# A Mamba-2 mixer on one core: one convolution tap of B and C moved to GpSimd, and eight smaller edits

## The chip, the cores and the metric

The kernel runs on one core of a Trainium2 chip. The core has five engines that each work through their own instruction list and wait for one another by semaphores: PE (TensorE, the matrix engine; PEld is its weight load), DVE (VectorE), ACT (ScalarE), POOL (GpSimd) and SP, which here only issues DMA transfers. Work that several engines share goes through SBUF (the 128-partition memory) and PSUM (8 banks of 128 x 512 float32, written by PE, not readable by POOL). The metric is the device time of one execution in microseconds (us).

## What is computed

```python
x  = hidden_states                                 # 2 x 512 tokens x 512
xn = layernorm(x)
out = x + mamba2(xn) + ffn(xn)
# mamba2: 128 heads of 64, state 128, 8 groups of B and C, causal conv of 4 taps, chunks of 128 tokens
gate, hBC, dt = split(xn @ in_proj_w.T)            # 8192, 8192 + 2*1024, 128
hs, B, C = split(silu(conv4(hBC) + conv_b))        # each channel: 4 taps along the tokens
dt = softplus(dt + dt_bias); A = -exp(A_log)
y = chunked state-space scan(hs*dt, A*dt, B, C) + D*hs
y = y * silu(gate); y = rmsnorm over each eighth of the 8192 channels (8 groups) * norm_weight
mamba2 = y @ out_proj_w.T
# ffn: xn @ W.T + b, plus one of 4 low-rank updates per token (ranks 8..64), chosen by a softmax gate
```

All matrix products of the projections are done in three passes over split operands: `xTh`, `wh` hold rounded values (fp32r), `xTl`, `wl` what the rounding left.

## The kernel before

The kernel is a hand-written program with one instruction list per engine, in which every order is the order of the code. For each of the two batches `b` (512 tokens, held as 4 chunks of 128, index `j`) it goes through these stages.

- **First tokens.** DVE computes mean and variance (`stats`, `mv`, `ve`), POOL the inverse deviation (`rstd`), DVE the normalized tokens `xn` (their memory is that of `gt`, so the trace calls them gt). PE turns them into PSUM (`turn_tokens`), ACT and DVE split them into `xTh` and `xTl` (`token_hi`, `token_lo`). For the second batch this is done inside the last steps of the first.
- **dt, gate of the feed-forward part, feed-forward part.** PE projects `dt` (`project_dt`) and the low-rank part (`project_ag`); DVE computes the softplus by a series with one multiply-add per coefficient (`soft_log`, constant `SERIES`) and the choice of rank (`route`), whose result `um` PE turns for ACT to copy (`uT`). `project_ffn` is 48 matmuls into the four output banks `bo`.
- **The B/C stage.** A loop over the 8 groups `g`. PE projects B of the group (unit u = 0, bank `bh` or `bt`) and C (u = 1, bank `bg` or `by`). The convolution of a unit is: ACT writes the newest tap with the bias from PSUM to `cv[:, u]` (`last_tap`), DVE adds the three older taps to it (`tap`, L820), ACT writes the tanh half of the silu to the PSUM bank (`tanh_conv`, L307), DVE multiplies (`silu_conv`, L826) into `h2` (B) or `ct` (C). Then PE multiplies B and C (`scores`, L640, one bank, `bo[2]`) and turns B (L644), and DVE masks the scores (`mask_scores`, L960) into `gt`. Two things order this loop: `cv` has two halves, one for B and one for C, so `last_tap` waits until the silu of the same half of the group before has read it; and `scores` waits for the mask of the scores before, since both use `bo[2]`:

```python
def last_tap(un, u, src):
    act.wait_ge(v_h2, did(un - 2))
...
def scores(b, g):
    pe.wait_ge(v_h2, did(b * UNITS + 2 * g + 1))
    pe.wait_ge(v_g, did(n - 1))
```

- **The 64 steps.** A loop over `m`, software-pipelined over three values of m: PE projects two heads and their gate (24 matmuls, L583), forms the output of step m-2 (12 matmuls, L726), the states, the scan and the turned channels of step m-1 (L770, L778, L786, L798). After each 8 steps (a norm group, `PER_GROUP`) the four banks `bo` hold the group's part of the output: DVE scales and adds two of them to `acc` (`add_group`, L846), ACT scales the other two into `part` (`drain`, L339) and POOL adds those (`add_drained`, L505).

SP issues loads in the order of the code too; weights of the B/C stage and of the steps pass through a two-deep buffer `raw`, from which ACT makes `wh` (`split_hi`) and POOL `wl` (`split_lo`).

Of the kernel before, what the change touches and what calls it, by code (L numbers as in the profile page):

```python
# [13 lines left out]
P = 128  # L14
# [17 lines left out]
SERIES = [1.0 / (2 * k + 1) for k in range(8)]  # L32
# [12 lines left out]
PRO_DVE_LOG = PRO_DVE_XT + 12  # L45
PRO_DVE_SC = PRO_DVE_LOG + 4
PRO_DVE_UM = PRO_DVE_SC + 16
PRO_DVE_CS = PRO_DVE_UM + 3
PRO_DVE_DTT = PRO_DVE_CS + 1
PRO_DVE_DTD = PRO_DVE_DTT + 1  # L50
PRO_DVE = PRO_DVE_DTD + NJ
CONST, SCALED = 6, 3
# [3 lines left out]
def mixer_kernel(nc, x, w_step, w_bc, w_dtag, w_out, par, headpar, w_ffn, w_b, b_ffn, b_gate, out):  # L56
    with ExitStack() as ctx:
# [57 lines left out]
        part = sb("part", [P, 2, HID])  # L115
# [28 lines left out]
        csT, dtT, ecT = xg[:, 0], xg[:, 1], tg[:, :]  # L144
        dec, dtd = yo[:, :], S[:, :, :].rearrange("p c k -> p (c k)")
# [8 lines left out]
        ld_const, const_ok, scaled = sem("ld_const"), sem("const_ok"), sem("scaled")  # L154
# [42 lines left out]

        def dtag(b):

            return b * LOADS  # L200
# [12 lines left out]

        block = ctx.enter_context(nc.Block())

        @block.sync
        def _(sp):
# [5 lines left out]
            load_x(0)  # L223
            sp.dma_start(par_sb[:, :, :], par).then_inc(ld_const, 16)
            sp.dma_start(hp[:, :], headpar).then_inc(ld_const, 16)
            for h in range(2):
                sp.dma_start(w_b_sb[MAXR * h:MAXR * (h + 1), :], w_b).then_inc(ld_const, 16)
            sp.dma_start(b_row[:, :], b_ffn.unsqueeze(0).broadcast_to([P, HID])).then_inc(ld_const, 16)
            sp.dma_start(bg_row[:, :], b_gate.unsqueeze(0).broadcast_to([P, NR])).then_inc(ld_const, 16)
# [7 lines left out]
            def store(b):  # L237
                last = b * GROUPS + (GROUPS - 1)
                blocks = out[b].rearrange("(j p) d -> p j d", p=P)
                if b + 1 < NB:  # L240
                    sp.wait_ge(v_acc, did(last, 2))
                    sp.wait_ge(p_acc, did(last, 2))
                    sp.dma_start(blocks, acc[:, b, :, :]).then_inc(st_out, 16)
                else:
                    for j in range(NJ):
                        sp.wait_ge(v_acc, did(last, 2, j + 1))
                        sp.dma_start(blocks[:, j, :], acc[:, b, j, :]).then_inc(st_out, 16)

            load(dtag(0))
            for b in range(NB):  # L250
                sp.wait_ge(a_ex, did(b * STEPS - 1))
                sp.dma_start(raw_f, w_ffn).then_inc(ld_ffn, 16)
                if b == 0:
                    load(bc(0, 0))
                load(bc(b, 1))
                if b == 0:
                    load_x(1)
# [33 lines left out]
        def _(act):  # L291
            start(act, (a_dr, a_tap, a_th, a_tg, a_rl, a_ex, a_s1, a_xh, a_sq, a_wh, a_wn, a_woh, a_bt))
            act.wait_ge(ld_const, 96)
# [11 lines left out]
            def tanh_conv(un, u, dst):  # L305
                act.wait_ge(v_tap, did(un, 3))
# [39 lines left out]
            for b in range(NB):  # L346
# [8 lines left out]
                if b == 0:  # L355
                    split_ffn(0)
# [769 lines left out]
```

## Time and profile before

| | |
|---|---|
| median of 3 runs | 1664.31 us (1662.31 to 1664.91) |
| the profiled execution | 1666.25 us, its span from first to last instruction 1664.5 us |
| mean granted TensorE clock | 0.994 of full speed |
| busy share of the span | PE 98%, PEld 82%, DVE 84%, ACT 75%, POOL 68% |
| HBM traffic | 207 MB read, 126 GB/s over the span |

In the profile's rows a timeline line gives the start, the busy time of one or several instructions in a row, the engine, the line of the kernel, the operation, the tiles it writes and reads, the count, and in brackets how long the engine had been idle and who released it. Times are us from the start of the span.

### The profile page before, as it was taken

The numbers are of one execution on the slowest core, as the hardware profiler recorded it, in microseconds if no ns is written. First come the engines' busy times: TensorE is split into PE (matmuls) and PEld (weight loads), VectorE is DVE, ScalarE is ACT, GpSimd is POOL, SyncE is SP. The second block draws the span as 40 slices with busy tenths as digits, with TensorE's granted clock in tenths as the row PEclk, the third lists the DMA queues.
The fourth block names the chain that finished last, engine by engine and source line by source line (L and its number), as shares of the span: only waits on it lengthen the run. The fifth ranks groups of instructions, "written<-read, shape, count | busy, mean of one in ns | idle before, by whom it ended". The sixth has DMA issues, their size and how long they took to land.

```text
span 1664.5 us, 28889 instructions
## 1 busy us (share of the span) xinstructions
PE 1625.2 (98%) x9638; PEld 1357.8 (82%) x9638; DVE 1394.8 (84%) x2361; ACT 1253.7 (75%) x2474; POOL 1130.0 (68%) x1442
## 2 busy tenths in 40 slices
PE   6999999999999999999899999999999999999998
PEld 4778888888888888888777788888888888888886
DVE  6888888888888888888879888888888888888887
ACT  3478788787888787887735787878887887878784
POOL 5237776767776777767653487777677777677674
PEclk9999999999999999999999999999999999999999
DMA  4244444344444344444313444444444444434431
GB/s 156 76 135 130 127 145 133 123 146 126 130 146 129 129 144 132 124 146 125 117 39 114 145 125 132 145 127 129 146 123 133 143 128 130 146 123 134 146 112 59
DMA packets 82307, 212.17 MB, mean 127 GB/s; under 512 B 11120, under 2 KB 27504, under 8 KB 81904
## 3 DMA queue, kind: packets, MB, share of 16 engines
q1 hardware_dynamic: 82160, 210.33, 40.0%
q8 instruction: 78, 1.28, 0.3%
q14 instruction: 69, 0.57, 0.1%
HBM read 207.14 MB, written 3.15 MB: 126 GB/s over the span
## 4 chain that ended last, share of the span: by engine, by line
PE 91%; DVE 4%; POOL 2%; ACT 1%; issue 1%; DMA 0%; SPq 0%; ACTq 0%; DVEq 0%; POOLq 0%
PE bg L583 21%; PE bo L726 21%; PE bt L583 11%; PE bh L583 11%; PE by L778 7%; PE bg L798 6%; PE bh L770 3%; PE bt L770 2%; PE bh L786 2%; PE bt L786 2%; DVE cv L820 1%; PE by L583 1%; PE bo L583 1%; PE bo L640 1%; PE bg L705 1%
## 5 line engine op out<-in xcount | busy, mean ns | idle before, releaser
L549 POOL TENSOR_TENSOR xl<-xg,xh 128x256 fp32r<-128x256 f32 x254 | 291.5, 1169 | 351.5 <-ACT xh L407 350.3
L483 POOL TENSOR_TENSOR wl<-raw,wh 128x256 fp32r<-128x256 f32 x584 | 424.3, 757 | 112.7 <-ACT wh L298 112.7
L311 ACT ACTIVATE mt<-cs_row,cs_tok 128x128 f32<-128x128 f32 x1024 | 324.6, 391 | 0.0
L563 POOL TENSOR_TENSOR wol<-raw_o,woh 128x256 fp32r<-128x256 f32 x256 | 181.4, 730 | 40.9 <-ACT woh L441 40.9
L726 PE MATMUL bo<-woh,xh 128*128 128x512 f32 x512 | 201.8, 394 | 2.1 <-POOL xl L549 2.1
L1034 DVE TENSOR_TENSOR mt<-mt,gt 128x1024 f32<-128x1024 f32 x128 | 202.8, 1584 | 0.4 <-ACT mt L450 0.4
L726 PE MATMUL bo<-woh,xl 128*128 128x512 f32 x512 | 200.9, 392 | 0.0
L726 PE MATMUL bo<-wol,xh 128*128 128x512 f32 x512 | 200.8, 392 | 0.0
L820 DVE SCALAR_TENSOR_TENSOR cv<-bt,par_sb,cv 128x511 f32<-128x511 f32 (+2 forms) x216 | 160.9, 745 | 12.4 <-ACT cv L302 7.3
L820 DVE SCALAR_TENSOR_TENSOR cv<-bh,par_sb,cv 128x511 f32<-128x511 f32 (+2 forms) x216 | 160.9, 745 | 6.7 <-ACT cv L302 1.6
L556 POOL TENSOR_TENSOR sqa<-sqa,sq 128x256 f32<-128x256 f32 x222 | 159.0, 736 | 1.2 <-ACT sq L424 1.2
L298 ACT ACTIVATE wh<-raw 128x1024 fp32r<-128x1024 f32 (+1 forms) x146 | 152.1, 1042 | 0.7 <-DMA raw<-in_w_dtag 0.7
L407 ACT ACTIVATE xh<-xg 128x512 fp32r<-128x512 f32 x128 | 81.0, 633 | 94.6 <-DVE xg L1011 94.6
L583 PE MATMUL bg<-xTh,wh 128*128 128x512 f32 (+1 forms) x552 | 148.2, 390 | 1.6 <-DVE yo L1003 1.6
L583 PE MATMUL bg<-xTh,wl 128*128 128x512 f32 (+1 forms) x552 | 147.9, 390 | 0.0
L583 PE MATMUL bg<-xTl,wh 128*128 128x512 f32 (+1 forms) x552 | 147.6, 389 | 0.0
L778 PE MATMUL by<-mt,xt 128*64 128x128 f32 x2032 | 139.0, 279 | 0.0
L450 ACT ACTIVATE mt<-mt 128x1024 f32<-128x1024 f32 x128 | 135.5, 1058 | 4.1
L583 PEld LDWEIGHTS bg<-xTh,wh 128*128 128x128 f32 (+1 forms) x552 | 102.8, 187 | 23.5 <-issue 1.3
L583 PEld LDWEIGHTS bg<-xTl,wh 128*128 128x128 f32 (+1 forms) x552 | 103.2, 187 | 22.0
L583 PEld LDWEIGHTS bg<-xTh,wl 128*128 128x128 f32 (+1 forms) x552 | 103.2, 187 | 22.0
L726 PEld LDWEIGHTS bo<-woh,xh 128*128 128x128 f32 x512 | 96.4, 188 | 30.0 <-POOL xl L549 3.8
(179 smaller groups left out, 3549.1 us busy)
## 6 DMA issues: line engine op xcount, KB each, us to landing
raw<-in_w_step SPq DMA_DIRECT2D x128, 512.0 KB, 3.5
cs_row<-cs_rows SPq DMA_DIRECT2D x128, 512.0 KB, 5.4
raw_o<-in_w_out SPq DMA_DIRECT2D x128, 256.0 KB, 4.0
ec_row<-ec_rows SPq DMA_DIRECT2D x256, 96.0 KB, 4.7
raw<-in_w_bc SPq DMA_DIRECT2D x16, 512.0 KB, 3.5
acc<-in_x SPq DMA_DIRECT2D x4, 512.0 KB, 4.7
cs_row<-in_w_ffn SPq DMA_DIRECT2D x2, 1024.0 KB, 5.9
out_dram<-acc SPq DMA_DIRECT2D x1, 1024.0 KB, 6.2
```

Of the source, the lines that this page charges most:

```text
L298: act.activation(wh[:, n % 2, 0:width(n)], raw[:, n % 2, 0:width(n)], ACT.Copy).then_inc(a_wh, 1)
L311: e = act.activation(mt[:, m % 2, h, chunk(j)], cs_row[:, m % 2, h, chunk(j)], ACT.Relu, bias=cs_tok[:, j, 2 * m + h:2 * m + h + 1], scale ...
L450: act.activation(mt[:, u], mt[:, u], ACT.Exp, scale=-1.0).then_inc(a_ex, 1)
L483: e = pool.tensor_tensor(wl[:, n % 2, cols], raw[:, n % 2, cols], wh[:, n % 2, cols].bitcast(F32), ALU.subtract)
L549: e = pool.tensor_tensor(xl[:, u, cols], xg[:, u, cols], xh[:, u, cols].bitcast(F32), ALU.subtract)
L556: e = pool.tensor_tensor(sqa[:, cols], sqa[:, cols], sq[:, cols], ALU.add)
L563: e = pool.tensor_tensor(wol[:, 1 - u, cols], raw_o[:, 1 - u, cols], woh[:, 1 - u, cols].bitcast(F32), ALU.subtract)
L583: mm = pe.matmul(dst, a(k), c(k), start=(n == 0 and k == 0), stop=(stop and n == 2 and k == KT - 1))
L726: mm = pe.matmul(bo[j][:, :], a[:, u, chunk(j)], c[:, u, :], start=(first and k == 0), stop=False, skip_group_check=True)
L778: mm = pe.matmul(yb[HD * h:HD * (h + 1), chunk(j)], xt[:, j, HD * h:HD * (h + 1)], mt[:, 1 - u, h, chunk(j)], start=True, stop=True)
L820: dve.scalar_tensor_tensor(out=cv[:, u, k:], in0=src[:, 0:L - k], scalar=par_sb[:, un % UNITS, TAPS - 1 - k:TAPS - k], in1=cv[:, u, k:], o ...
L1034: dve.tensor_tensor(mt[:, 1 - u], mt[:, 1 - u], gt[:, (m - 1) % GROUPS, :].unsqueeze(1).broadcast_to([P, 2, L]), ALU.mult).then_inc(v_m, 1)
```

## The change

It has nine parts.

1. **B/C taps.** In the B/C stage, ACT writes two taps instead of one: the newest into `cv[:, u]`, the second newest into a buffer of its own (`tap2`, the memory of `sq` and `sqa`). POOL adds the second to the first (`add_tap`), and DVE adds only the two oldest (`far_taps`), behind POOL. The steps keep the old way.
2. **Order in the B/C loop.** On DVE the silu of C of group g-1 now stands behind the far taps of B of group g, and the mask of group g-3 behind that; on ACT the tanh of C of group g-1 stands behind the two taps of B of group g. `decays` moves from g = 0 to g = 1 and `decays_to_end` from g = 1 to g = 3.
3. **Series.** `SERIES` has 6 coefficients instead of 8: two DVE operations on 512 columns fewer per batch.
4. **First loads.** SP loads the first weights before the parameters; the parameters have three semaphores of their own instead of one. `scale_consts` moves on POOL from the start to behind `split_ffn_lo`.
5. **Four banks.** The first batch's turned tokens go to `bo[0..3]`, so PE does not wait for the split of the first two; ACT splits the feed-forward weights earlier.
6. **Pre-multiplied identity.** PE does 12 matmuls of the identity with itself before its first wait.
7. **Norm of the second batch.** Its statistics were one block of DVE work at m = 61 and its `norm` two pairs at m = 62 and 63; now they are single instructions, in the steps m = 52 to 57 and m = 60 to 63, ahead of the state update.
8. **Three output blocks by ACT.** `DVE_BLOCKS = 1`: DVE adds one of the four blocks, ACT scales three, POOL adds three (two in one step and the third in the next).
9. **Last step.** In the last batch DVE takes the tokens and masks the decays of the last step ahead of the y chain.

The core of the diff:

```diff
-SERIES = [1.0 / (2 * k + 1) for k in range(8)]
+SERIES = (1.0, 0.33333333660263703, 0.1999985316596525, 0.14296178997116357, 0.10853287901120869, 0.11612164608329507)
+TOP = len(SERIES) - 1
+DVE_BLOCKS = 1
+ACT_BLOCKS = NJ - DVE_BLOCKS
+        tap2 = sq, sqa
...
# scalar
+            def two_taps(b, g, u, src):
+                un = b * UNITS + 2 * g + u
+                last_tap(un, u, src)
+                if g == 0 and u == 0:
+                    act.wait_ge(p_sqa, squares(b - 1, STEPS - 1))
+                elif g == 0:
+                    act.wait_ge(t_ss, did(b * GROUPS - 1))
+                else:
+                    act.wait_ge(p_cv, did(bc_unit(b, g - 1, u)))
+                act.activation(tap2[u][:, :], src[:, :], ACT.Identity,
+                               scale=par_sb[:, un % UNITS, TAPS - 2:TAPS - 1]).then_inc(a_t2, 1)
...
-                act.wait_ge(p_acc, did(g - 1, 2))
-                for j in (2, 3):
-                    act.activation(part[:, j - 2, :], bo[j][:, :], ACT.Identity, scale=rr[:, j:j + 1]).then_inc(a_dr, 1)
+                act.wait_ge(p_acc, did(g - 1, ACT_BLOCKS))
+                for j in range(DVE_BLOCKS, NJ):
+                    act.activation(part[:, j - DVE_BLOCKS, :], bo[j][:, :], ACT.Identity, scale=rr[:, j:j + 1]) \
+                        .then_inc(a_dr, 1)
...
                 for g in range(GROUPS):
                     act.wait_ge(t_b, did(b * GROUPS + g))
-                    last_tap(b * UNITS + 2 * g, 0, bank_b[g % 2])
+                    two_taps(b, g, 0, bank_b[g % 2])
+                    if g >= 1:
+                        tanh_bc(b, g - 1, 1, bank_c[(g - 1) % 2])
+                    if g >= 3:
+                        take_b(b, g - 3)
                     act.wait_ge(t_c, did(b * GROUPS + g))
-                    last_tap(b * UNITS + 2 * g + 1, 1, bank_c[g % 2])
+                    two_taps(b, g, 1, bank_c[g % 2])
                     split_hi(bc(b, g + 2))
...
-                    tanh_conv(b * UNITS + 2 * g, 0, bank_b[g % 2])
-                    tanh_conv(b * UNITS + 2 * g + 1, 1, bank_c[g % 2])
+                    tanh_bc(b, g, 0, bank_b[g % 2])
# gpsimd
             def scale_consts():
                 pool.wait_ge(scaled, 1)
+                pool.wait_ge(ld_par, 32)
...
+            def add_tap(b, g, u):
+                pool.wait_ge(a_t2, did(bc_unit(b, g, u)))
+                for cols in (slice(1, 257), slice(257, L)):
+                    e = pool.tensor_tensor(cv[:, u, cols], cv[:, u, cols],
+                                           tap2[u][:, cols.start - 1:cols.stop - 1], ALU.add)
+                e.then_inc(p_cv, 1)
...
                     inverse_dev(0)
-                    pool.wait_ge(ld_const, 96)
-                    scale_consts()
                     split_lo(dtag(0))
-                if b == 0:
                     split_lo(bc(0, 0))
                     split_ffn_lo(0, 0)
                 split_ffn_lo(b, 1)
+                if b == 0:
+                    scale_consts()
...
-                for g in range(2, GROUPS):
-                    split_lo(bc(b, g))
+                for g in range(GROUPS):
+                    for u in range(2):
+                        add_tap(b, g, u)
+                    if g + 2 < GROUPS:
+                        split_lo(bc(b, g + 2))
# tensor
+            for i in range(WARM):
+                pe.matmul(by[:, chunk(i % NJ)], ident[:, :], ident[:, :], start=True, stop=True)
...
-                    mm = pe.transpose(bank_t[j % 2][:, chunk(k)], xn[:, j, chunk(k)], ident[:, :])
+                    mm = pe.transpose(bank_x(b, j)[:, chunk(k)], xn[:, j, chunk(k)], ident[:, :])
# vector
+            def far_taps(b, g, u, src):
+                q, un = bc_unit(b, g, u), b * UNITS + 2 * g + u
+                for k in (2, 3):
+                    if k == 2:
+                        dve.wait_ge(p_cv, did(q))
+                    else:
+                        dve.wait_ge(v_bc, did(q, 2, 1))
+                    dve.scalar_tensor_tensor(out=cv[:, u, k:], in0=src[:, 0:L - k],
+                                             scalar=par_sb[:, un % UNITS, TAPS - 1 - k:TAPS - k], in1=cv[:, u, k:],
+                                             op0=ALU.mult, op1=ALU.add).then_inc(v_bc, 1)
...
-                    for k in range(1, TAPS):
-                        tap(un, 0, bank_b[g % 2], k)
-                    for k in range(1, TAPS):
-                        tap(un + 1, 1, bank_c[g % 2], k)
+                    far_taps(b, g, 0, bank_b[g % 2])
+                    if g >= 1:
+                        silu_conv(un - 1, 1, bank_c[(g - 1) % 2], ct[:, g - 1, :])
+                    if g >= 3:
+                        mask_scores(b, g - 3)
+                    far_taps(b, g, 1, bank_c[g % 2])
...
                     silu_conv(un, 0, bank_b[g % 2], h2[:, g % 2, :])
-                    silu_conv(un + 1, 1, bank_c[g % 2], ct[:, g, :])
-                    if g == 0:
+                    if g == 1:
+                        add_lora(b)
                         decays(b)
-                    if g >= 2:
-                        mask_scores(b, g - 2)
...
+                    ahead = m == STEPS and b + 1 == NB
+                    if ahead:
+                        take_tokens()
+                        mask_decays()
...
+                    if b + 1 < NB and STEPS - 12 <= m < STEPS - 6:
+                        h, part_of = divmod(m - (STEPS - 12), 3)
+                        if part_of < 2:
+                            stats_of(b + 1, 2 * h + part_of)
+                        else:
+                            variance(b + 1, h)
+                    if b + 1 < NB and STEPS - NJ <= m < STEPS:
+                        norm(b + 1, m - (STEPS - NJ))
```

How DVE's list stands at group g = 2 of the first batch before the change (cv is the convolution buffer, h2 and ct are B and C after the silu, gt the masked scores; the wait names are semaphores, a_ of ACT, v_ of DVE, p_ of POOL, t_ of PE):

```order
L820 SCALAR_TENSOR_TENSOR cv<-bh,par_sb,cv 128x511 [waits a_tap]
L820 SCALAR_TENSOR_TENSOR cv<-bh,par_sb,cv 128x510 [waits v_tap]
L820 SCALAR_TENSOR_TENSOR cv<-bh,par_sb,cv 128x509 [waits v_tap]
L820 SCALAR_TENSOR_TENSOR cv<-bg,par_sb,cv 128x511 [waits a_tap]
L820 SCALAR_TENSOR_TENSOR cv<-bg,par_sb,cv 128x510 [waits v_tap]
L820 SCALAR_TENSOR_TENSOR cv<-bg,par_sb,cv 128x509 [waits v_tap]
L826 SCALAR_TENSOR_TENSOR h2<-bh,cv 128x512 [waits a_th,t_bt]
L826 SCALAR_TENSOR_TENSOR ct<-bg,cv 128x512 [waits a_th]
L960 TENSOR_TENSOR gt<-bo2,causal 128x512 [waits t_gm]
```

The same place on DVE with the change (groups 2 and, from bt on, 3):

```order
L880 SCALAR_TENSOR_TENSOR cv<-bh,par_sb,cv 128x510 [waits p_cv,pro_dve]
L880 SCALAR_TENSOR_TENSOR cv<-bh,par_sb,cv 128x509 [waits v_bc]
L896 SCALAR_TENSOR_TENSOR ct<-by,cv 128x512 [waits a_th]
L880 SCALAR_TENSOR_TENSOR cv<-bg,par_sb,cv 128x510 [waits p_cv]
L880 SCALAR_TENSOR_TENSOR cv<-bg,par_sb,cv 128x509 [waits v_bc]
L896 SCALAR_TENSOR_TENSOR h2<-bh,cv 128x512 [waits a_th,t_bt]
L880 SCALAR_TENSOR_TENSOR cv<-bt,par_sb,cv 128x510 [waits p_cv]
L880 SCALAR_TENSOR_TENSOR cv<-bt,par_sb,cv 128x509 [waits v_bc]
L896 SCALAR_TENSOR_TENSOR ct<-bg,cv 128x512 [waits a_th]
L1037 TENSOR_TENSOR gt<-bo2,causal 128x512 [waits t_gm]
```

Each unit has lost its first tap, the first of the two left waits for POOL (p_cv), the two silus are no longer neighbours, and the mask stands in the group after.

ACT's list at group g = 2 of the first batch, before:

```order
L302 ACTIVATE cv<-bh,par_sb 128x512 [waits v_h2,t_b]
L302 ACTIVATE cv<-bg,par_sb 128x512 [waits v_h2,t_c]
L298 ACTIVATE wh<-raw 128x1024 [waits ld_raw1]
L307 ACTIVATE bh<-cv 128x512 [waits v_tap]
L307 ACTIVATE bg<-cv 128x512 [waits v_tap]
```

and with the change (sq and sqa are the memory of the second tap):

```order
L320 ACTIVATE cv<-bh,par_sb 128x512 [waits v_h2,t_b]
L337 ACTIVATE sq<-bh,par_sb 128x512 [waits p_cv]
L342 ACTIVATE by<-cv 128x512 [waits v_bc]
L320 ACTIVATE cv<-bg,par_sb 128x512 [waits v_h2,t_c]
L337 ACTIVATE sqa<-bg,par_sb 128x512 [waits p_cv]
L316 ACTIVATE wh<-raw 128x1024 [waits ld_raw1]
L342 ACTIVATE bh<-cv 128x512 [waits v_bc]
```

The second tap has come in behind the first, and the tanh of C of group 1 (by) has moved behind the taps of B of group 2.

POOL's list at the same place had only the four pieces of `wl` per group (L483); with the change two units of two additions stand between them:

```order
L522 TENSOR_TENSOR wl<-raw,wh 128x256 [waits a_wh]
L522 TENSOR_TENSOR wl<-raw,wh 128x256 x3
L529 TENSOR_TENSOR cv<-cv,sq 128x256 [waits a_t2]
L529 TENSOR_TENSOR cv<-cv,sq 128x255
L529 TENSOR_TENSOR cv<-cv,sqa 128x256 [waits a_t2]
L529 TENSOR_TENSOR cv<-cv,sqa 128x255
```

So POOL now stands between ACT's taps and DVE's for every unit.

## Rows read from the trace of the kernel before

**Rows 1.** Windows: PE, PEld, DVE, ACT, POOL busy (count), PEclk, DMA share, GB/s.
```profile
110.00:800.00 690.00, 689.46 (x4192) 579.13 (x4191) 583.55 (x995) 555.46 (x1111) 503.51 (x633) 1.00 0.43 134
```

**Rows 2.** Timeline of PE, the step after a norm group's end.
```profile
209.11 1.17 PE L583 MATMUL bh<-xTh,wh 128*128 128x512 f32 x4
...
219.72 1.41 PE L798 MATMUL bg<-ct,S 128*128 128x128 f32 x6
220.89 1.17 PE L583 MATMUL bt<-xTh,wh 128*128 128x512 f32 x4
...
232.06 1.17 PE L583 MATMUL bh<-xTh,wh 128*128 128x512 f32 x4
```

**Rows 3.** Timeline of DVE, then of ACT, in that step.
```profile
212.26 1.40 DVE L846 SCALAR_TENSOR_TENSOR acc<-bo,rr,acc 128x512 f32<-128x512 f32 x2
...
219.61 0.98 DVE L853 SCALAR_TENSOR_TENSOR S<-S,cd_bc,bt 128x64 f32<-128x64 f32 x4 [0.70 <-ACT S L444]
...
211.85 1.24 ACT L339 ACTIVATE part<-bo,rr 128x512 f32<-128x512 f32 x2
```

**Rows 4.** Timeline of ACT, then of DVE, B/C stage, group 2.
```profile
61.13 0.78 ACT L302 ACTIVATE cv<-bh,par_sb 128x512 f32<-128x512 f32 x1 [3.04 <-DVE h L826]
...
64.17 2.31 DVE L820 SCALAR_TENSOR_TENSOR cv<-bg,par_sb,cv 128x511 f32<-128x511 f32 x3
...
67.75 0.68 DVE L960 TENSOR_TENSOR gt<-bo,causal 128x512 f32<-128x512 f32 x1
```

**Rows 5.** The page, part 5: a two-input addition on POOL.
```profile
L556 POOL TENSOR_TENSOR sqa<-sqa,sq 128x256 f32<-128x256 f32 x222 | 159.0, 736 | 1.2 <-ACT sq L424 1.2
```

**Rows 6.** Timeline of PE, B/C stage: first batch, then second.
```profile
60.49 1.16 PE L640 MATMUL bo<-ct,h 128*128 128x128 f32 x8 [1.66 <-DVE acc L985]
...
64.58 1.07 PE L583 MATMUL by<-xTh,wh 128*128 128x512 f32 x4
...
881.25 2.08 PE L640 MATMUL bo<-ct,h 128*128 128x128 f32 x8 [3.19 <-DVE acc L985]
...
888.08 1.07 PE L583 MATMUL by<-xTh,wh 128*128 128x512 f32 x4
```

**Rows 7.** Windows behind two idle stretches of PE.
```profile
33.60:37.00 3.40, 3.40 (x10) 2.68 (x9) 2.72 (x11) 1.48 (x4) 1.64 (x3) 0.53 0.19 36
...
881.20:887.20 6.00, 5.96 (x20) 5.20 (x21) 5.55 (x9) 2.99 (x4) 2.80 (x4) 0.51 0.00 0
```

**Rows 8.** Timeline of DVE, then of PE, first batch before the steps.
```profile
22.77 0.43 DVE L895 TENSOR_SCALAR mt<-mt 128x512 f32<-128x512 f32 x1 [7.38 <-ACT mt L331]
...
29.23 4.37 DVE L904 SCALAR_TENSOR_TENSOR bt<-bt,sg 128x512 f32<-128x512 f32 x6
...
38.27 2.98 DVE L935 TENSOR_TENSOR gt<-ag,msk 128x64 f32<-128x64 f32 x4
...
48.12 0.68 DVE L942 SCALAR_TENSOR_TENSOR sg<-tg,mt 128x512 f32<-128x512 f32 x1
...
50.62 0.43 DVE L948 TENSOR_SCALAR xg<-sg 128x512 f32<-128x512 f32 x1
...
57.95 2.48 DVE L985 TENSOR_TENSOR acc<-bo,acc 128x512 f32<-128x512 f32 x4
...
60.95 0.68 DVE L826 SCALAR_TENSOR_TENSOR ct<-by,cv 128x512 f32<-128x512 f32 x1
...
32.52 1.20 PE L583 MATMUL bo<-xTh 128*128 128x512 f32 x4 [3.29 <-POOL xTl L494]
...
109.23 1.18 PE L583 MATMUL bt<-xTh,wh 128*128 128x512 f32 x4
```

**Rows 9.** Timeline of PE, steps 62 and 63 of the first batch.
```profile
799.62 1.17 PE L583 MATMUL bh<-xTh,wh 128*128 128x512 f32 x4
...
813.68 1.17 PE L583 MATMUL bt<-xTh,wh 128*128 128x512 f32 x4
```

**Rows 10.** Timeline of PE, last step.
```profile
1647.30 0.91 PE L770 MATMUL bt<-xd,btok 128*128 128x128 f32 x6 [3.13 <-DVE xt L1025]
```

More of the change, by code:

```diff
@@ L196, in bank_y, with bc_unit @@
             return bh if b + 1 == NB and m == STEPS - 1 else by
+        def bc_unit(b, g, u):
+            return 2 * (b * GROUPS + g) + u
         def dtag(b):
@@ L212, in chunk, with bank_x @@
             return slice(P * c, P * (c + 1))
+        def bank_x(b, j):
+            return bo[j] if b == 0 else bank_t[j % 2]
         block = ctx.enter_context(nc.Block())
@@ L568, in _ @@
                     if has(m - 2) and m > 2 and (m - 2) % PER_GROUP == 0:
-                        add_drained(b, (n - 2) // PER_GROUP - 1)
+                        add_drained(b, (n - 2) // PER_GROUP - 1, range(ACT_BLOCKS - 1))
+                    if has(m - 2) and m > 3 and (m - 3) % PER_GROUP == 0:
+                        add_drained(b, (n - 3) // PER_GROUP - 1, (ACT_BLOCKS - 1,))
                     if 2 <= m < 2 + NJ:
@@ L841, in add_group @@
                 else:
-                    dve.wait_ge(p_acc, did(g - 1, 2))
-                for j in range(NJ if very_last else 2):
+                    dve.wait_ge(p_acc, did(g - 1, ACT_BLOCKS))
+                for j in range(NJ if very_last else DVE_BLOCKS):
                     if very_last:
@@ L939, in route, with add_lora @@
                 assert done[b] == PRO_DVE_UM
+            def add_lora(b):
+                dve.wait_ge(pe_, b * PRO_PE + PE_LORA)
+                for j in range(NJ):
+                    tick(b, dve.tensor_tensor(acc[:, b, j, :], bo[j][:, :], acc[:, b, j, :], ALU.add))
+                assert done[b] == PRO_DVE_LORA
             def decays(b):
@@ L965, in _ @@
                 if b == 0:
-                    norm_stats(0)
+                    for h in range(2):
+                        stats_of(0, 2 * h)
+                        stats_of(0, 2 * h + 1)
+                        variance(0, h)
                     for j in range(NJ):
@@ L1028, in _, with mask_decays @@
                                           ALU.mult).then_inc(v_x, 1)
-                    if ended is not None:
-                        add_group(b, ended)
-                    if has(m - 1):
+                    def mask_decays():
                         dve.wait_ge(a_ex, did(n - 1))
@@ L1036, in _ @@
                                           ALU.mult).then_inc(v_m, 1)
+                    ahead = m == STEPS and b + 1 == NB
+                    if ahead:
+                        take_tokens()
+                        mask_decays()
+                    if has(m - 2):
+                        y_chain()
+                    if m == STEPS and b + 1 < NB:
+                        token_lo(b + 1, 0)
+                        token_lo(b + 1, 1)
+                    if has(m - 1) and not ahead:
+                        take_tokens()
+                    if ended is not None:
+                        add_group(b, ended)
+                    if has(m - 1) and not ahead:
+                        mask_decays()
                     if m == STEPS and b + 1 < NB:
@@ L1066, in _ @@
                                                  op0=ALU.mult, op1=ALU.add).then_inc(v_y1, 1)
-                    if b + 1 < NB and m == STEPS - 3:
-                        norm_stats(b + 1)
-                    if b + 1 < NB and STEPS - 2 <= m < STEPS:
-                        for j in range(2):
-                            norm(b + 1, 2 * (m - (STEPS - 2)) + j)
             dve.wait_ge(a_xh, did(NB * STEPS - 1))
```

171 lines of the change are left out of this document (90 added, 81 removed).

## The prediction

> **What bounds the kernel now.** I read three views. First the table of busy time by stretches: in the steps of the first batch PE works 689.46 of 690 us at full clock [rows 1], so there PE is the limit, and no edit of another engine can give time back except where PE still waits. So I looked, second, at the timeline of PE for steps longer than their neighbours, and third at the B/C stages and the passage between the batches, where the other engines set the pace.
>
> A plain step takes 11.17 us (220.89 to 232.06). The step behind a norm group's end takes 11.78 (209.11 to 220.89), and the reader sees why in L798: its matmuls are spread over 1.41 us, since they wait for the states [rows 2]. DVE makes these states at 219.61, behind 1.40 us for two output blocks at 212.26 [rows 3]. There are 14 such steps, m = 10, 18, ... 58 in both batches. The other long step is m = 62: 14.06 us (799.62 to 813.68) [rows 9], because the statistics of the second batch stand there in one block on DVE.
>
> In the B/C stage before, DVE is nearly always busy: three taps of one unit take 2.31 us, a silu and a mask 0.68 each [rows 4, 8]. PE needs 4.09 us for a group's scores, the turning of B and its first projection (60.49 to 64.58), and 2.7 for the second projection, 6.8 together [rows 6]. The two engines run about level, and from the end of the silu of C of group 1 (60.95 + 0.68 = 61.63) to step 1 (109.23) the stage takes 47.6 us [rows 8].
>
> **The change, part by part.**
>
> Group ends (part 8): DVE does one block of 0.70 instead of two of 1.40, so its taps and, by way of ACT, the states come 0.7 earlier, and PE's 0.61 of waiting (11.78 less 11.17) should go. ACT pays 0.62 more (half of 1.24) [rows 3] for the third block; its next tap is needed by DVE only behind the mask of the decays, so I hide it there. POOL pays two pieces of 0.736 [rows 5] in the step after; it is idle in 27% of the steps [rows 1]. 14 x 0.61 = **-8.5**. From below: 0, if ACT is late instead.
>
> Norm of the second batch (part 7): each single instruction (0.5 to 0.65 us) falls in DVE's idle time ahead of the states, 0.70 even in the crowded step [rows 3]. Step 62 comes back to a plain one: 14.06 less 11.17 = **-2.9**. If the gaps did not hold them, up to half of it would return.
>
> Start (parts 3 to 6). DVE began the softplus at 22.77 [rows 8]. It waits for `scale_consts`, which now stands on POOL behind the splits of B/C weights (4 pieces) and of the feed-forward weights (8 pieces). ACT should have fed the former at about 13.9, an estimate from the tokens' turning without its two waits; 12 pieces of 0.736 and 0.9 for the constants end at 23.6. So the earlier tokens don't reach DVE: +0.8. Two coefficients fewer give 2 x 0.73 (4.37 over 6) = -1.5. `route` ended at 38.27 + 2.98 = 41.25 and now ends at 40.6. PE's wait of 3.29 ahead of the feed-forward part [rows 8] goes, but PE then waits for `route`. The 12 identity matmuls lie in time in which PE has no data; I give them nothing.
>
> **B/C stage (parts 1 and 2), the term that decides.** DVE's work per group falls from six taps to four. But look at what follows what. `last_tap` of B of group g+1 waits for the silu of B of group g, since `cv` has only one half for B. Before, DVE then still had the silu of C and the mask to do, and the ACT tap (0.78, at 61.13, right behind DVE's h) [rows 4] was covered. Now the silu of C stands on DVE behind the far taps of B of the next group, and these wait for POOL, which waits for ACT, which waits for the silu just done. So DVE is idle for all of ACT's and POOL's part, and the same again for C. One half-turn is: ACT two taps 1.30 (0.78 and a second like the 0.62 of L339, less overlap) [rows 3, 4]; POOL two pieces of 0.736, 1.47 [rows 5]; DVE two of three taps, 2/3 of 2.31 = 1.54, and a silu 0.68 [rows 4, 8]; three hand-overs of 0.07 (PE starts at 60.49 behind DVE's 57.95 + 2.48) [rows 6, 8]. Sum **5.2**, so **10.4 us per group** where PE needs 6.8. From below it is bounded by PE's pace, 3.4 a half-turn; from above by 6.0, if POOL's additions grow as its pieces do under DVE's load.
>
> Walking it: far taps of group 0 end 3.1 behind `route`, 43.7; silu 44.4; two half-turns to the silu of B of group 1, 54.8; then `add_lora` 2.48 and `decays` 2.93 (48.12 to 51.05) [rows 8], 60.2; far taps and silu of C of group 1 at 62.4. That was 61.63. From here 11 half-turns, 57.2, lead to the silu of B of group 7: 119.6. In the first of them PE waits for the first mask, which now comes a group later, over 8 us; behind such an idle stretch the same work takes 6.83 us (881.25 to 888.08) instead of 4.09 [rows 6], with the granted clock at 0.51 and 0.53 [rows 7], the lower level of 1.2 GHz. Less a slack of 0.36 (5.2 against 0.68 + 0.07 + 4.09) this costs 2.4: 122.0. Then silu and mask 1.4, scores and gate 4.1, and tanh, product, silu and turning 2.6: step 1 at 130.1 against 109.23 [rows 8], **+20.9**. The second batch has the same loop; I take the same, **+41.8** for both.
>
> Clock: each later turn leaves PE idle for 10.4 less 6.8 = 3.6 us. Idle stretches of 3.29 [rows 8] and 3.19 [rows 6] were both followed by the lower level [rows 7], the one of 1.66 was not [rows 6]. Each drop can put up to 2.4 into the turn. Some three idles per batch are of this length; I take two drops for each batch, 4 x 2.4, **+10** rounded, between 0 and 17.
>
> The Trainium skill ("TensorE: Matmul & The Clock Gate", section "HAM oscillation") says that a loop whose every turn holds an idle wait of PE pays the slow clock in every turn, and this speaks against the change. By it the time would be that of the third rival below; the trace agrees in that both long idles were followed by 0.51 to 0.53.
>
> Last step (part 9): PE's wait of 3.13 [rows 10] shrinks by some 2, but ACT's copy of the state stands behind `xh`, which waits for the y chain that has moved back; PE gets its state no earlier. 0, within 1 both ways.
>
> Sum: -8.5 - 2.9 + 41.8 + 10 = **+40.4**. The profiled execution took 1666.25 us, 1.75 more than its span of 1664.5; the median of the runs is 1.9 below it. On the median: 1664.3 + 40.4 = **1704.7**.
>
> **The rivals.**
> - The clock does not drop beyond the first time: -10, 1695. For it: PE's idle of 3.6 may be cut by the turn's own second wait. 18%.
> - ACT's third block makes a new wait at the group ends, so that nothing is won there: +8.5, 1713. For it: ACT's list is in order, and its tap is 0.62 later. Against: DVE comes to that tap late itself. 10%.
> - The clock drops in every turn, four more per batch: 8 x 2.4 = 19 in place of 10, 1714. 20%.
> - The other side: the half-turn is covered after all, because DVE finds enough other work, and the stage runs at PE's 6.8. Then about 3 us come back per batch and the sum is -17, 1647. It decides where a half-turn falls below 3.9 (then 11 of them per batch eat just the 11.4 won elsewhere). Against it: 1.30, 1.47, 1.54 and 0.68 are durations of instructions that follow one another by semaphores. 5%.
>
> **How the numbers follow.** My forecast has 45%, and 2% is left for the rest. The range takes in the first and third rival, a half-turn shorter or longer by 0.4 (22 x 0.4 = 9), and the start's uncertainty of 2: 1687 to 1720. A change of this kernel under 0.2% can't be told from none. Faster by more: 5%; within: 1%; slower: 94%.
>
> **What would show it.** On the timeline: a silu of B every 10.4 us in the B/C stage, with DVE idle behind POOL (L529) twice per group, some 2.9 us each; PE waiting 3 to 4 us per group for the mask, and clock stretches near 0.5 there; step 1 at about 130; steps behind group ends at 11.2; step 62 at 11.2. Wrong would be the whole if the far taps of a unit started without waiting for POOL, if B/C groups passed in under 8 us, or if the steps themselves grew longer.

## The result, and the profile after

The changed kernel takes 1707.95 us (median of 4 runs, 1707.65 to 1713.1) beside 1663.9 us (1662.31 to 1664.91) of the kernel before on the same chip: the ratio is 1.0272, with a 95% interval of 1.0256 to 1.0288, so it is 44 us slower. The prediction was 1704.7, range 1687 to 1720. The profiled execution of the changed kernel is the longest of its four: 1713.1 us, with a span of 1711.3 and a granted clock of 0.978 (the others 0.980 to 0.982); places read from its trace hold up to 5.2 us more than the median.

Where the 46.8 us between the two spans lie can be read from one instruction of PE at four places, its first projection pass of a step. First the two rows of the timeline of the kernel before that are not among those above (step 1 of the second batch, and the last `ct,S` pass before the last step):

```profile
931.34 1.17 PE L583 MATMUL bt<-xTh,wh 128*128 128x512 f32 x4
...
1643.34 0.83 PE L798 MATMUL bg<-ct,S 128*128 128x128 f32 x6
```

The same places and the two plain comparisons in the timeline of PE after:

```profile
138.71 1.17 PE L637 MATMUL bt<-xTh,wh 128*128 128x512 f32 x4
...
328.93 1.17 PE L637 MATMUL bh<-xTh,wh 128*128 128x512 f32 x4
...
340.07 1.17 PE L637 MATMUL bt<-xTh,wh 128*128 128x512 f32 x4
...
824.91 1.17 PE L637 MATMUL bh<-xTh,wh 128*128 128x512 f32 x4
...
836.11 1.17 PE L637 MATMUL bt<-xTh,wh 128*128 128x512 f32 x4
...
981.76 1.17 PE L637 MATMUL bt<-xTh,wh 128*128 128x512 f32 x4
...
1690.00 0.83 PE L856 MATMUL bg<-ct,S 128*128 128x128 f32 x6
```

Step 1 of the first batch starts 138.71 - 109.23 = 29.5 us later [rows 8]. A step behind a group's end takes 340.07 - 328.93 = 11.14 and not 11.78 [rows 2], step 62 takes 11.20 and not 14.06 [rows 9]; so at the end of step 62 the delay is down to 836.11 - 813.68 = 22.4. Passage and B/C stage of the second batch add 28.0 (981.76 - 931.34 = 50.4), its steps give 3.8 back (1690.00 - 1643.34 = 46.7), and the last step changes nothing (46.8 at the end). All of the loss lies in the two B/C stages with what leads to them.

One turn of the B/C stage after, in the second batch, shows the loop. DVE, then ACT, then POOL:

```profile
938.96 1.53 DVE L880 SCALAR_TENSOR_TENSOR cv<-bt,par_sb,cv 128x510 f32<-128x510 f32 x2 [2.99 <-POOL cv L529]
940.41 0.68 DVE L896 SCALAR_TENSOR_TENSOR ct<-bg,cv 128x512 f32<-128x512 f32 x1
941.00 0.68 DVE L1037 TENSOR_TENSOR gt<-bo,causal 128x512 f32<-128x512 f32 x1
944.08 1.53 DVE L880 SCALAR_TENSOR_TENSOR cv<-by,par_sb,cv 128x510 f32<-128x510 f32 x2 [2.40 <-POOL cv L529]
...
949.20 1.53 DVE L880 SCALAR_TENSOR_TENSOR cv<-bh,par_sb,cv 128x510 f32<-128x510 f32 x2 [2.98 <-POOL cv L529]
...
941.18 0.78 ACT L320 ACTIVATE cv<-by,par_sb 128x512 f32<-128x512 f32 x1 [2.86 <-DVE ct L896]
941.86 0.68 ACT L337 ACTIVATE sqa<-by,par_sb 128x512 f32<-128x512 f32 x1
...
942.62 1.43 POOL L529 TENSOR_TENSOR cv<-cv,sqa 128x256 f32<-128x256 f32 x2 [3.69 <-ACT sqa L337]
```

Read it as a circle: DVE's silu of C ends at 941.09, ACT's first tap of the next C begins at 941.18, POOL follows at 942.62, DVE's far taps at 944.08. From far taps to far taps it is 5.12 us, 10.24 for a group, and DVE idles 2.99 + 2.40 us in it.

PE in the first batch, its waits in that stage and what ran behind two of them:

```profile
76.17 2.04 PE L694 MATMUL bo<-ct,h 128*128 128x128 f32 x8 [7.85 <-DVE gt L1037]
...
98.74 1.13 PE L694 MATMUL bo<-ct,h 128*128 128x128 f32 x8 [2.51 <-DVE gt L1037]
...
108.98 2.04 PE L694 MATMUL bo<-ct,h 128*128 128x128 f32 x8 [3.30 <-DVE gt L1037]
...
121.86 2.05 PE L694 MATMUL bo<-ct,h 128*128 128x128 f32 x8 [3.07 <-DVE gt L1037]
...
126.86 2.07 PE L637 MATMUL bh<-xTh,wh 128*128 128x512 f32 x4 [2.31 <-POOL wl L522]
```

The turn (from one group's scores to the next) from 98.74 takes 10.24 us, the one from 108.98 takes 12.88. Windows behind that wait and behind one of 2.53 us in the second batch (the granted clock is the seventh of the figures behind the window, the one ahead of the DMA share):

```profile
108.90:114.90 6.00, 5.92 (x20) 5.18 (x21) 2.09 (x3) 2.22 (x4) 1.41 (x2) 0.50 0.00 0
946.00:951.00 5.00, 2.77 (x13) 1.96 (x11) 1.98 (x4) 2.26 (x4) 2.25 (x4) 1.00 0.56 205
```

The last row of PE is a wait that the prediction does not have: POOL's split of the weights of step 0.

### The profile page after: what moved, and what is told of

Same layout as the page of the kernel before. It is cut to its first block, busy times and chain, and to the rows that moved or that the text cites. A ratio compares the mean times of both kernels' runs of the same rounds, so it can differ in the third digit from the quotient of the medians.

```text
span 1711.3 us, 29035 instructions
## 1 busy us (share of the span) xinstructions
PE 1640.0 (96%) x9662; PEld 1372.6 (80%) x9662; DVE 1367.5 (80%) x2310; ACT 1284.3 (75%) x2521; POOL 1194.8 (70%) x1536
## 4 chain that ended last, share of the span: by engine, by line
PE 82%; DVE 7%; POOL 6%; issue 2%; ACT 2%; DMA 0%; POOLq 0%; DVEq 0%; ACTq 0%
PE bg L637 19%; PE bo L783 19%; PE bh L637 11%; PE bt L637 10%; PE by L836 7%; PE bg L856 5%; PE bh L828 2%; PE bt L828 2%; PE bh L844 2%; PE bt L844 2%; DVE cv L880 2%; POOL cv L529 2%; POOL wl L522 1%; ACT cv L320 1%; POOL xl L599 1%
## 5 line engine op out<-in xcount | busy, mean ns | idle before, releaser
L890 DVE SCALAR_TENSOR_TENSOR cv<-bh,par_sb,cv 128x511 f32<-128x511 f32 (+2 forms) x192 | 143.0, 745 | 15.7 <-ACT cv L320 11.1
L890 DVE SCALAR_TENSOR_TENSOR cv<-bt,par_sb,cv 128x511 f32<-128x511 f32 (+2 forms) x192 | 143.0, 745 | 6.2 <-ACT cv L320 1.7
L836 PEld LDWEIGHTS by<-mt,xt 128*64 128x64 f32 x2032 | 108.3, 136 | 15.3
```

Of the source, the lines that this page charges most:

```text
L836: mm = pe.matmul(yb[HD * h:HD * (h + 1), chunk(j)], xt[:, j, HD * h:HD * (h + 1)], mt[:, 1 - u, h, chunk(j)], start=True, stop=True)
L890: dve.scalar_tensor_tensor(out=cv[:, u, k:], in0=src[:, 0:L - k], scalar=par_sb[:, un % UNITS, TAPS - 1 - k:TAPS - k], in1=cv[:, u, k:], o ...
```

## The experiments

Twelve kernels, each compared with the kernel before on its chip. Medians in us; the ratio is to the kernel before, with its 95% interval. The changed kernel is 1707.95, 1.0272 (1.0256 to 1.0288). Where two of these kernels ran on different chips, the ratios are the safer comparison.

**1. Which chain makes the turn of 10.2 us?** Three kernels: four places for the sum of the taps in place of two; the mask moved; both.

```
+ def tapped(g, u, cols=slice(0, L)):
+     return cv[:, u, cols] if g % 2 == 0 else part[:, u, cols]
```
```
+ if g >= 3:
+     mask_scores(b, g - 3)
  far_taps(b, g, 0, bank_b[g % 2])
  if g >= 1:
      silu_conv(un - 1, 1, ...)
- if g >= 3:
-     mask_scores(b, g - 3)
```

> The changed kernel (median 1707.95 us), with four places for the sum of the taps in place of two in the B/C stage: odd groups sum in the room of `part`, so the first tap of a unit no longer waits for the silu of the group before. Nothing of the computation changes. Theory of the prediction, the wait for the place alone makes the half-turn of 5.1 us: with it gone the stage runs at PE's 6.8 us per group, about 11 half-turns x 1.7 us and the clock drops come back in each batch, 1655 to 1665 us. Rival, a second chain of the same length runs through PE: projection of B, ACT 1.30, POOL 1.42, DVE far taps 1.53, silu of C 0.68, mask 0.68, scores, turning and the next projection 4.09 and three hand-overs of 0.07, 9.9 us per group: the time falls by only 0 to 6 us, 1702 to 1708.

> The changed kernel with the mask of group g-3 moved ahead of the far taps of B of group g on DVE; two places for the sum as before. Nothing of the computation changes. Theory of the prediction, the half-turn through the place in cv sets the pace: it stays at 5.1 us, PE only waits at another point, 1702 to 1708 us (what comes back are clock drops, at most 2.4 each). Rival, the chain through the mask and PE alone sets the pace: 6.8 to 8 us per group, 1660 to 1675.

> Both together: four places for the sum and the mask ahead of the far taps of B. If the pace is set by the longer of the two chains, each of about 10 us, only this one of the three is fast: PE's 6.8 us per group, 1645 to 1657 us (the other parts of the change are worth about 12 us against the kernel before). If GpSimd's tap or its share of a port is the cause, the time stays above 1690.

Measured: four places 1686.65 (1.0126, 1.0111 to 1.0141), mask ahead 1699.1 (1.0203, 1.0188 to 1.0218), both 1657.55 (0.9951, 0.9936 to 0.9966). The masks in the timeline of DVE with four places alone:

```profile
80.03 0.68 DVE L1043 TENSOR_TENSOR gt<-bo,causal 128x512 f32<-128x512 f32 x1
90.06 0.68 DVE L1043 TENSOR_TENSOR gt<-bo,causal 128x512 f32<-128x512 f32 x1
```

and with the mask ahead alone:

```profile
90.55 0.68 DVE L1037 TENSOR_TENSOR gt<-bo,causal 128x512 f32<-128x512 f32 x1
100.76 0.68 DVE L1037 TENSOR_TENSOR gt<-bo,causal 128x512 f32<-128x512 f32 x1
```

10.0 us a group in the one, 10.2 in the other: there are two chains of nearly the same length, and each edit takes away only one. The chain of the prediction runs through the place in `cv`; the second runs from the projection of B through ACT, POOL and DVE to the mask, and from there through PE's scores to the next projection of B. Its length of 9.9 had been worked out ahead of the run and came as 10.0. The times of the single edits fell into neither of the two ranges that each expectation names: they gave 21 and 9 us. Two things in their traces go that way: the first mask comes earlier (68.56 and 70.12 where the changed kernel has 75.34), and less runs at the lower clock (mean granted clock 0.989 and 0.986 in place of 0.978); how much each is worth was not separated. With the mask ahead alone, part of the gain is also lost again at the end of the stage, where PE waits 7.86 us for POOL's split of the weights of step 0 (experiment 2). With both chains cut the time is 0.55 us above the expected range of 1645 to 1657; PE has no wait for a mask between its groups, and its scores follow one another in 6.7 us. Timeline of PE with the mask ahead alone, then with both:

```profile
121.88 2.07 PE L637 MATMUL bh<-xTh,wh 128*128 128x512 f32 x4 [7.86 <-POOL wl L522]
```
```profile
80.39 1.06 PE L699 MATMUL bo<-ct,h 128*128 128x128 f32 x8
...
87.10 1.05 PE L699 MATMUL bo<-ct,h 128*128 128x128 f32 x8
```

**2. What is left in that kernel.**

```profile
99.62 2.07 PE L642 MATMUL bh<-xTh,wh 128*128 128x512 f32 x4 [4.45 <-POOL wl L527]
```

Four places and mask ahead, timeline of PE: 4.45 us for POOL's split of the weights of step 0, which the change put behind the taps of group 7. The edit, alone on the changed kernel and on top of both others:

```
- if g + 2 < GROUPS:
+ if g + 2 <= GROUPS:
      split_lo(bc(b, g + 2))
...
- if m >= -1 and (has(m + 1) ...): split_lo(step(b, m + 1))
+ if m >= 0 and (has(m + 1) ...): split_lo(step(b, m + 1))
```

> The kernel of four_mask (1657.55 us) with one more edit: GpSimd splits the weights of step 0 behind the taps of group 6, no longer behind those of group 7. In the trace of four_mask PE waited 4.45 us for this split ahead of step 0 and ran at the lower level behind it. If this wait is the rest of what separates it from the gains of the other parts: 2 x 4.45 and some of the slow passes behind come back, 1645 to 1650 us. If step 0 is held by the taps of group 7 as well, little: 1654 to 1658.

> The changed kernel with GpSimd's split of the weights of step 0 behind the taps of group 6 in place of group 7, and nothing else. PE's wait of 2.31 us for it comes back in each batch, 2 x 2.3, or up to 2 x 4 if the following passes run faster too: 1700 to 1704 us. If the chain through DVE sets the start of the steps anyway: 1707 to 1708.

Measured: 1649.8 (0.9906, 0.9891 to 0.9921) on top of both, as expected; 1699.47 (1.0203, 1.0188 to 1.0218) alone, 8.5 us less than the changed kernel and 0.5 us under the expected range of 1700 to 1704. The wait explains 2 x 2.3 of these 8.5. In the first batch of this trace PE also kept its full clock behind two idle stretches like those that the lower clock followed in the changed kernel; in the second batch it did not (rows in the last section). So the rest is put down to the clock; no run shows it apart.

**3. Order or tap?** The two parts undone one at a time, and both. Undoing the order puts `silu_conv` of B and C and the mask of group g-2 behind both `far_taps`; undoing the tap is

```
- for k in (2, 3):
+ for k in (1, 2, 3):
```

in `far_taps`, with ACT's second tap and POOL's `add_tap` left out.

> The changed kernel with the old order of the B/C stage on DVE and ACT (both far taps, then both silus, then the mask of group g-2), the tap on GpSimd and two places kept. Nothing of the computation changes. If the order is what costs: the chains of B and C run beside each other, 6.5 us from silu of B to silu of B, which is under PE's 6.8; 1648 to 1662 us. If the tap on GpSimd itself costs, through its two more hand-overs per unit or by slowing DVE: 1685 to 1705.

> The changed kernel with the tap on GpSimd undone and the new order kept: DVE does three taps of a unit again, ACT one, two places. Nothing of the computation changes. Half-turn by the place: ACT 0.78, DVE 2.31 and 0.68, two hand-overs of 0.07, 3.9 us, so 7.8 a group; the chain through the mask and PE: 0.78, 2.31, 0.68, 0.68, 4.09 and three hand-overs, 8.75 a group. By the longer, 1.5 us per group less than the changed kernel's 10.2, and no idle stretch of PE over 3 us: 1675 to 1690. If the tap on GpSimd were the whole cause: 1648 to 1658; if the order alone were: 1700 or more.

> The changed kernel with the order and the tap on GpSimd both undone in the B/C stage; everything else of the change is kept (start, spread norm, third block on ACT, last step). By the terms of the prediction, -8.5 for the group ends, -2.9 for the norm and about -1 for the start: 1664 - 12 = 1652, between 1648 and 1656. If one of the other parts costs something that the B/C stage hid: above 1660.

Measured: old order with the tap on GpSimd 1662.96 (0.9982, 0.9973 to 0.9992), 1 us above what was expected if the order is what costs; new order with DVE's own taps 1671.11 (1.003, 1.0018 to 1.0042), 4 us under its expected 1675; neither 1648.42 (0.9897, 0.988 to 0.9913), within what was expected. Over the last one the order alone costs 23 us, the tap alone 15, both together 60: some 22 us appear only where both are present. In the trace of the old order PE waits 4.36 us for POOL's `wl` ahead of step 0 of the first batch and 4.37 in the second, 8.7 of the 15; and the turning of `um` begins at 41.46 in place of 38.63, 2.8 more (experiment 5 shows why). Timeline of PE:

```profile
101.88 2.08 PE L634 MATMUL bh<-xTh,wh 128*128 128x512 f32 x4 [4.36 <-POOL wl L519]
```
 In the trace of the new order with own taps DVE's masks are 8.7 us apart, the 8.75 worked out for the second chain:

```profile
86.71 0.68 DVE L1027 TENSOR_TENSOR gt<-bo,causal 128x512 f32<-128x512 f32 x1
95.43 0.68 DVE L1027 TENSOR_TENSOR gt<-bo,causal 128x512 f32<-128x512 f32 x1
```

**4. The clock.** More work for PE ahead of two waits; its results are unused.

```
+ if g in (4, 5):
+     pe.wait_ge(pa, b * PRO_ACT + ACT_TABD)
+     for i in range(6):
+         pe.matmul(bo[1][:, chunk(i % NJ)], ident[:, :], ident[:, :], start=True, stop=True)
  pe.wait_ge(v_g, did(n - 1))
```

> The changed kernel with six more matmuls of the identity on TensorE ahead of the waits for the mask in the scores of groups 4 and 5; their results are not used. In the trace of the changed kernel PE idled 3.30 and 3.07 us there, the passes behind took up to 2.05 us in place of 1.17, and the turn behind the first of the two took 12.9 us in place of 10.2. If the idle stretch brings the slow clock, the first of the two turns is 10.2 again in both batches, 2 x 2.6; the second gives nothing, since PE then waits for GpSimd's split of the weights: 1702 to 1704 us. If the slow passes have another cause: 1707 to 1709, or more if the six matmuls delay the scores.

Measured: 1705.79 (1.024, 1.0225 to 1.0256), where the kernel before took 1665.86 in the same comparison and 1663.9 in that of the changed kernel. By the ratios the gain is 0.0032 x 1664 = 5.3 us, by the medians 2.2; the intervals touch, so its size is not settled, its sign is likely. By the median it lies between the two ranges of the expectation, in neither. The trace of the first batch:

```profile
106.17 1.50 PE L695 MATMUL bo<-ident 128*128 128x128 f32 x12
109.51 1.16 PE L698 MATMUL bo<-ct,h 128*128 128x128 f32 x8 [1.85 <-DVE gt L1041]
...
119.73 1.16 PE L698 MATMUL bo<-ct,h 128*128 128x128 f32 x8 [1.90 <-DVE gt L1041]
...
124.80 2.07 PE L637 MATMUL bh<-xTh,wh 128*128 128x512 f32 x4 [3.58 <-POOL wl L522]
```

The turn is 10.22 and not 12.88, and the scores take 1.16 and not 2.04; the same holds in the second batch (10.24 and 1.16). The second filled turn only makes PE wait longer for POOL, as expected. This fits the idle stretch as the cause, but one profiled execution doesn't prove it: in the trace of experiment 5 the unfilled waits at the same places kept the full clock too (last section).

**5. GpSimd beside `route`.** In the changed kernel POOL runs the taps of group 0 while DVE is in the small operations of `route`.

```
  def add_tap(b, g, u):
+     if g == 0 and u == 0:
+         pool.wait_ge(pv, b * PRO_DVE + PRO_DVE_UM)
```

> The changed kernel with one more wait: GpSimd's first tap of a batch waits for the end of `route` on DVE. In the changed kernel the six last small operations of `route` took 0.67 us each while GpSimd ran the taps of group 0, and 0.18 each with GpSimd idle in the kernel with order and tap undone (4.09 us for six against 1.11). If GpSimd's work beside them is the cause, `route` ends near 38.7 us in place of 41.06, PE idles 2.9 us and not 5.1 ahead of the turning of um, and the far taps of group 0 begin near 40.2: 1702 to 1706 us. If they are slow for another reason, `route` still ends at 41.06 and the taps come 1.4 us later in each batch: 1709 to 1712.

Timeline of DVE, the changed kernel and then this one:

```profile
35.44 1.34 DVE L1001 TENSOR_TENSOR seen<-seen,eq 128x4 f32<-128x4 f32 x2
36.81 2.00 DVE L1003 SCALAR_TENSOR_TENSOR msk<-seen,msk 128x4 f32<-128x4 f32 x3
38.85 2.18 DVE L1006 TENSOR_TENSOR gt<-ag,msk 128x64 f32<-128x64 f32 x4
```
```profile
34.60 0.37 DVE L1003 TENSOR_TENSOR seen<-seen,eq 128x4 f32<-128x4 f32 x2
35.00 0.56 DVE L1005 SCALAR_TENSOR_TENSOR msk<-seen,msk 128x4 f32<-128x4 f32 x3
35.60 1.27 DVE L1008 TENSOR_TENSOR gt<-ag,msk 128x64 f32<-128x64 f32 x4
```

Measured: 1704.91 (1.0234, 1.0219 to 1.0249), within what was expected; its interval ends just below that of the changed kernel, so there is a gain, of 3.0 us by the medians and 6.3 by the ratios. The mechanism is shown by the rows: 0.67 us for an operation on 4 columns beside POOL, 0.18 alone, and `route` ends at 36.9 in place of 41.0. The expectation had 38.7, so more was regained at that place than it had.

**6. The third output block on ACT**, undone on the kernel with order and tap undone.

```
- DVE_BLOCKS = 1
+ DVE_BLOCKS = 2
```

POOL then adds its two blocks in one step.

> The kernel of both_back (1648.42 us) with two output blocks on DVE and two on ACT at the group ends, as in the kernel before. By the term of the prediction the steps behind group ends are 11.78 us again in place of 11.15, 14 x 0.61: 1656 to 1658. If ACT's third block had cost something of its own: less, 1652 to 1655.

Measured: 1656.76 (0.9946, 0.9931 to 0.9961), 8.3 us more than 1648.42; a step behind a group's end is 217.35 - 205.57 = 11.78 again:

```profile
205.57 1.17 PE L622 MATMUL bh<-xTh,wh 128*128 128x512 f32 x4
...
217.35 1.18 PE L622 MATMUL bt<-xTh,wh 128*128 128x512 f32 x4
```

**7. The constants scaled earlier**, on the kernel with order and tap undone.

```
  split_lo(bc(0, 0))
+ scale_consts()
  split_ffn_lo(0, 0)
```

> The kernel of both_back (1648.42 us) with the scaling of the constants on GpSimd ahead of the splits of the feed-forward weights in place of behind them. There DVE waited 8.91 us for it and began the softplus at 22.10; ACT's input was ready at 18.3. DVE gains 3.7 us, of which PE, which ends the feed-forward part at 35.7, can take the 2.87 that it idled ahead of the turning of um, and up to 1.9 of passes that ran slow behind that idle stretch: 1643.5 to 1646. If `route` only ends against other work that comes later: 1648.

Measured: 1646.61 (0.9884, 0.9868 to 0.9901), the lowest median here, but only 1.8 us less than 1648.42, with overlapping intervals and 0.6 us above the expected range: a gain is not shown. DVE's softplus began at 20.10 and not at the 18.4 that the expectation counts on, since the wait moved from POOL to the projection of `dt` on PE, whose passes took 1.94 and 1.91 us in this execution and 1.17 and 1.08 in the one it was worked out from:

```profile
20.10 0.85 DVE L951 TENSOR_SCALAR mt<-mt 128x512 f32<-128x512 f32 x1 [6.85 <-ACT mt L358]
```
```profile
13.39 1.94 PE L623 MATMUL bh<-xTh,wh 128*128 128x512 f32 x4 [1.83 <-DVE xTl L943]
15.13 1.91 PE L623 MATMUL bh<-xTl,wh 128*128 128x512 f32 x4
```

## Why the prediction held, step by step

- **The half-turn of the B/C stage** was the term that decides, and it was right in mechanism and size: 5.2 us predicted, 5.12 measured, with ACT 1.4 (0.78 and 0.68, overlapping), POOL 1.43, DVE 1.53 and 0.68. What the prediction did not see is that a second chain, through the mask and PE, is just as long (10.0 us a group). It didn't matter to the number, but it matters to the cure: removing the buffer wait alone leaves the stage at 10.0 (experiment 1).
- **Its cost per batch** was put too low: step 1 was to start at 130.1 and started at 138.71. The missing 8.6 us are the silu of C of group 1 at 65.2 and not 62.4 (2.8), PE's wait for POOL ahead of step 0 (2.3), and 3.5 that are left for the clock, which the prediction had in a term of its own. With that wait moved (experiment 2, alone), step 1 started at 130.12. For both stages together the prediction had 41.8 + 10 = 51.8 us, the trace has 57.5, and the comparison of the changed kernel with the one with both parts undone gives (1.0272 - 0.9897) x 1664 = 62.
- **POOL's new wait** is the step that was missed: the listing of the change showed the split of step 0 behind the last taps, and the prediction asked of DVE and PE what they wait for, not of POOL what stands behind `add_tap`. It costs 2.3 us a batch here, 4.4 where the loop is cut, and 7.9 with the mask ahead alone.
- **The clock**: two further drops for each batch were assumed, and the trace has two (at 108.98 and 121.86, in the second batch at 952.07 and 964.94). The slow passes at 126.86 belong to the second of them: the granted clock is 0.50 from 121.80 to 129.00, through the wait for POOL. The price of one was put at up to 2.4; the turn shows 2.6. That there are two is in part luck: no row stood behind "some three idles", the waits were 2.28 to 3.30 us and not 3.6 in every turn, and in other executions the count differs (last section). One more drop for each batch, at the scores of group 0 (59.76 and 902.84), was not foreseen and cost PE nothing that is seen, since it then waits 7.85 and 7.83 us for the first mask. The rival of a drop in every turn (1714) is out: the turns behind waits for a mask of 2.28 to 2.53 us kept their full clock in this trace.
- **Group ends** -8.5: the step came down by 0.64 each, and experiment 6 gives 8.3. **Norm** -2.9: 14.06 to 11.20. **Last step** 0: 46.7 before it, 46.8 behind it.
- **The start** was mis-sized in both directions. DVE began the softplus at 22.35 in place of the predicted 23.6. Without GpSimd's tap `route` ends at 38.6 in place of the predicted 40.6, so the other parts are worth 17 us (experiment 3) and not the 12 of the prediction; in its trace step 1 is 4.2 us earlier in the first batch, where 0.7 was forecast, and some 3.5 lie in the passage and the stage of the second batch, which no run separates. With GpSimd's tap beside it, `route` is slowed to 41.0 and PE idles 5.09 us and then runs at the lower clock, which is most of the 2.8 above. The errors of the gains and of the loss have opposite signs and leave 3 us in the sum; that they nearly cancel is luck.
- **The identity matmuls** were given nothing. The projection of `dt` behind them ran at 1.17 and 1.08 us a pass in this trace, and at 2.04 and 1.91 before; DVE then waited for POOL anyway (8.95 us at 22.35), so no time came of it there. They don't do it each time: of the 13 traces of kernels with these matmuls, all three passes took under 1.2 us in four, and in nine at least one took 1.7 us or more (as in experiment 7).

## What to carry to other kernels

When work moves to another engine, count the chain once more for every resource that closes it: the buffer, and also the engine that produces the next input; here two chains of 10 us stood side by side, and either cure alone looked weak. Taking work off a busy engine gains nothing when the new order puts its own consumer behind the hand-over: DVE lost a third of its taps and idled 5.4 of 10.2 us. Then read the queue of the helping engine: what stood behind the added instructions (here the split of the next weights) is late by their length.

## What the runs showed of the hardware that was not expected

Small operations on DVE slow down beside GpSimd: 0.18 us each for 4 columns alone, 0.67 each while POOL ran its two-input additions (experiment 5). Not all of them do. Timeline of DVE in the second batch of the kernel with order and tap undone, where POOL worked without a gap from 838.80 to 848.61:

```profile
842.42 0.62 DVE L982 TENSOR_TENSOR pr<-ex,rse 128x16 f32<-128x16 f32 x1
843.08 0.17 DVE L983 TENSOR_REDUCE psel<-pr 128x4 f32<-128x16 f32 x1
843.29 0.18 DVE L984 RECIPROCAL rpsel<-psel 128x4 f32<-128x4 f32 x1
843.50 0.23 DVE L985 TENSOR_TENSOR msk<-psel,rpsel 128x4 f32<-128x4 f32 x1
843.77 0.69 DVE L986 COPY seen<-eq 128x4 f32<-128x4 f32 x1
```

The first one with two inputs is slow, and so is the copy; the reduction and the reciprocal, with one input, aren't. The second with two inputs took only 0.23. The slow ones and this one end at 843.04, 843.73 and 844.46, some 0.7 us apart like POOL's pieces, which fits a wait for the end of POOL's piece: an operation that comes late in a piece waits little. The Trainium skill ("SBUF — State Buffer", section "SBUF: two separate sides") says that GpSimd and a DVE operation with two SBUF inputs exclude each other for the whole instruction, and the same for one in a 2-port mode; the trace agrees (whether the copy ran in such a mode no row shows), with up to 0.7 us for 0.17, about one piece of POOL's 0.71. The far taps, whose one input lies in PSUM, kept their 1.53 us for two (at 944.08 of the changed kernel, with POOL at work from 944.00).

The length of an idle stretch of PE alone does not tell whether the lower clock follows. In the changed kernel 3.30 us was followed by 0.50. With POOL's split moved (experiment 2, alone), two stretches of 3.29 us in the first batch were not, but one of 3.26 in the second was. In the kernel of experiment 5 one of 2.50 was, but the next of 3.08 was not. Timeline of PE, the kernel of experiment 2 and then that of experiment 5:

```profile
107.35 1.13 PE L694 MATMUL bo<-ct,h 128*128 128x128 f32 x8 [3.29 <-DVE gt L1037]
117.58 1.13 PE L694 MATMUL bo<-ct,h 128*128 128x128 f32 x8 [3.29 <-DVE gt L1037]
...
943.05 2.04 PE L694 MATMUL bo<-ct,h 128*128 128x128 f32 x8 [3.26 <-DVE gt L1037]
```
```profile
94.03 2.05 PE L696 MATMUL bo<-ct,h 128*128 128x128 f32 x8 [2.50 <-DVE gt L1039]
105.52 1.13 PE L696 MATMUL bo<-ct,h 128*128 128x128 f32 x8 [3.08 <-DVE gt L1039]
```

So the clock term of such a kernel is a spread of several us, here between executions of one kernel too (1707.65 and 1713.1), and not a number. The Trainium skill ("TensorE: Matmul & The Clock Gate", section "HAM oscillation") describes a loop with a wait of some 3 to 5 us in every turn, which pays the slow clock in every turn. The waits here are at the short end of that or below it, and these traces show it in part only. In the three traces of the changed kernel, of experiment 2 alone and of experiment 5 there are, besides the first of each batch, 24 waits for a mask of 2.27 to 3.30 us; after 16 of them the scores took 1.13 us, after 8 they took 2.04 or 2.05. In the changed kernel it was 4 and 4, with all four waits over 3 us among the slow.
